# Exponential and inverse root of the attention stage on ScalarE, from one function table

## The reference, cut to what matters

```python
qk = x @ Wqk + bqk
v = x @ Wv + bv
scores = jnp.sum(qk[dst] * qk[src], axis=-1) / jnp.sqrt(jnp.float32(D))
scores = jnp.clip(scores, -5.0, 5.0)
m = jax.ops.segment_max(scores, dst, num_segments=N)
e = jnp.exp(scores - m[dst])
s = jax.ops.segment_sum(e, dst, num_segments=N)
attn = e / s[dst]
out = jax.ops.segment_sum(attn[:, None] * v[src], dst, num_segments=N)
out = out @ Wo + bo
h = out + x
mu = jnp.mean(h, axis=-1, keepdims=True)
var = jnp.mean(jnp.square(h - mu), axis=-1, keepdims=True)
return gamma * (h - mu) / jnp.sqrt(var + 1e-05) + beta
```

## Time and profile before

| | us |
|---|---|
| median of 3 runs | 3318.11 |
| lowest, highest | 3316.03, 3324.59 |
| the profiled execution | 3321.51 |
| its span, first to last instruction | 3319.7 |

### The profile page before, as it was taken

The page is one execution under the profiler, slowest core; times in us unless marked ns, Lnnn a source line. Parts: engine busy times, 40 slices in busy tenths (PEclk is TensorE's granted clock), DMA queues, the critical chain, the costliest instruction groups (busy, mean ns, idle before and its releaser), DMA issues. The chain is left out here.

```text
span 3319.7 us, 49065 instructions
## 1 busy us (share of the span) xinstructions
PE 2144.1 (65%) x10561; PEld 1502.5 (45%) x10561; DVE 2130.9 (64%) x8721; ACT 1682.1 (51%) x4589; POOL 1599.9 (48%) x1491
## 2 busy tenths in 40 slices
PE   0267353563775878777772777777885777773665
PEld 0123242252553656666650333333444666662555
DVE  1268842332886889898875777776754444441999
ACT  0149310122886556565654988988974444440222
POOL 0130046643001788888845655655515777775000
PEclk9779677777998677676775999999997888785999
DMA  7930142244999778787855999988985555541998
GB/s 312 346 103 6 48 86 37 69 115 90 325 325 315 250 240 245 239 251 237 247 131 159 284 270 278 295 266 262 301 197 188 186 186 184 181 158 71 312 317 283
DMA packets 494699, 696.78 MB, mean 210 GB/s; under 512 B 66363, under 2 KB 357398, under 8 KB 485932
## 3 DMA queue, kind: packets, MB, share of 16 engines
q1 hardware_dynamic: 414254, 485.35, 47.1%
q0 software_dynamic: 63360, 130.75, 14.8%
q10 hardware_dynamic: 16896, 78.91, 6.3%
HBM read 394.91 MB, written 327.18 MB: 218 GB/s over the span
## 5 line engine op out<-in xcount | busy, mean ns | idle before, releaser
L262 POOL DMA_INDIRECT xs<-x_d,table_src x400 | 385.2, 963 | 379.4 <-DVE x L1485 148.2
L262 POOL DMA_INDIRECT xs<-n_d,srcI x200 | 234.6, 1173 | 326.3 <-DVEq L1134 270.8
L262 POOL DMA_INDIRECT xd<-n_d,dstI x200 | 239.6, 1198 | 61.0 <-issue 54.9
L262 POOL DMA_INDIRECT xd<-x_d,table_dst x200 | 211.0, 1055 | 65.1 <-issue 65.1
L1699 POOL DMA_INDIRECT r_d<-rd,out_row x200 | 196.8, 984 | 61.3 <-issue 59.1
L1640 PE MATMUL bank<-nmsg,same 128*128 128x128 f32 x400 | 100.6, 335 | 149.7 <-ACT sums L1572 92.5
L1640 PEld LDWEIGHTS bank<-nmsg,same 128*128 128x128 f32 x400 | 61.8, 195 | 286.2 <-ACT sums L1572 223.1
L1822 PE MATMUL bank<-xs,same 128*128 128x129 f32 x400 | 106.4, 355 | 129.1 <-DVE same L1764 68.3
L518 PE MATMUL bank<-mask,h 128*128 128x512 f32 x160 | 104.1, 810 | 131.8 <-DVE mask L856 79.5
L452 POOL DMA_INDIRECT sum_d<-add,to x40 | 63.7, 1593 | 240.5 <-ACT add L647 226.9
L238 DVE RECIPROCAL rs<-root 128x4 f32<-128x4 f32 (+3 forms) x253 | 51.8, 205 | 193.0 <-ACT root L257 178.6
(11 more groups left out here) (382 smaller groups left out, 7173.8 us busy)
## 6 DMA issues: line engine op xcount, KB each, us to landing
n_d<-T SPq DMA_DIRECT2D x98, 528.0 KB, 3.8
nt<-n_d SPq DMA_DIRECT2D x49, 1056.0 KB, 7.0
r<-r_d SPq DMA_DIRECT2D x98, 520.0 KB, 5.5
bc<-dst_d SPq DMA_DIRECT2D x170, 256.0 KB, 4.8
r_d<-nv SPq DMA_DIRECT2D x49, 528.0 KB, 8.1
v_d<-nv SPq DMA_DIRECT2D x49, 528.0 KB, 7.8
nv<-v_d SPq DMA_DIRECT2D x49, 528.0 KB, 4.1
x_d<-x SPq DMA_DIRECT2D x100, 256.0 KB, 4.0
```

What stands on the lines that cost most here:

```text
L262: pool.indirect_dma_start(out=out, out_offset=None, in_=table, in_offset=bass.IndirectOffsetOnAxis(ap=index, axis=0)).then_inc(s, 16)
```

## The change

GpSimd's power, its constant `base` and its wait for the scores go. ScalarE takes the exponential of the score (`exps`) from its tables. The root and VectorE's reciprocal are replaced by two activations on ScalarE: `logs`, Ln of D-th of the sum plus eps, and `inverses`, Exp of minus half of that. One table set that holds Exp and Ln is loaded at the stage's start in the place of that of the root. On ScalarE, `exps` and `logs` stand ahead of `weigh` and `inverses` behind it.

```diff
-        base = sb("base", [P, G])
...
-                    nc.gpsimd.memset(base[:, :], math.e)
...
-                    def exps(g, s):
-                        hold("pool", pool, score_ready, g + 2)
-                        nc.gpsimd.tensor_tensor(e[:, s, :], base[:, :], score[:, s, :], ALU.pow).then_inc(e_ready, 1)
-                    unrolled(NGE, [(exps, 3), (src_used, S8), (dst_used, S8), (rows, 0)], S8)
+                    unrolled(NGE, [(src_used, S8), (dst_used, S8), (rows, 0)], S8)
...
-                    pipeline(dve, NGE, [(nodes_biased, 1, -1), (denominator, 6), (inverse, 2, late), (attended, 6), (offset, 2, late),
+                    pipeline(dve, NGE, [(nodes_biased, 1, -1), (denominator, 6), (attended, 6), (offset, 2, late),
                                         (nodes_stats, 1, -1), (sames, 3), (biased, 6), (scores, 2), (stats2, 6), (indices, 1),
                                         (nodes_summed, 1, -1), (attended_summed, 6), (differences, 1, late), (times_gamma, 7),
                                         (squares, 1, late), (nodes_gamma, 2, -1), (total, 1, late), (added, 7),
...
-                    act.preload_act_table(ACT.Sqrt)
+                    act.preload_act_table_set("natural_log_exp_and_others")
...
+                    def exps(g, s):
+                        act.wait_ge(score_ready, g + 2)
+                        nc.scalar.activation(e[:, s, :], score[:, s, :], ACT.Exp).then_inc(e_ready, 1)
...
-                    roots = rooting(act, tmp, root, mixed, rooted)
+
+                    def logs(k, s):
+                        act.wait_ge(mixed, k + 1)
+                        nc.scalar.activation(root[:, s, :], tmp[:, s % 2, 2, :], ACT.Ln, bias=eps[:, :], scale=1.0 / D).then_inc(rooted, 1)
+
+                    def inverses(k, s):
+                        act.wait_ge(rooted, k + 1)
+                        nc.scalar.activation(rs[:, s, :], root[:, s, :], ACT.Exp, scale=-0.5).then_inc(inverted, 1)
...
                     pipeline(act, NGE, [(hdT_copy, 2), (total(0), 4), (normed, 7), (total(1), 4), (nodes_normed(0), 2, -1),
-                                        (total(2), 4), (nodes_normed(1), 2, -1), (attT_copy, 5), (total(3), 4), (weigh, 3),
-                                        (roots, 1, late)], S8)
+                                        (total(2), 4), (nodes_normed(1), 2, -1), (attT_copy, 5), (total(3), 4), (exps, 3), (logs, 1, late),
+                                        (weigh, 3), (inverses, 1, late)], S8)
```

## The result

The changed kernel takes 3336.95 us (median of 4 runs, 3334.32 to 3339.46) against 3317.07 for the kernel before: the ratio is 1.0051, with a 95% interval of 1.0027 to 1.0076. It is slower, by half a per cent. The forecast was 3297 us. In some sets of measurements every kernel, the kernel before included, took 8 to 10% longer, so a time of the experiments means something only beside the kernel before of its own set (3319 or 3320 us in the one kind, 3587 to 3654 in the other).

A forecast was written before the change was run, and what follows sets the result against it. GpSimd was taken as the bound at 13.16 us a group; 12.6 after the change saves 21 us in 38 steady groups and 3 in the others, less 3 of drain: 3297 us, forecast span 3283 to 3308, eight in ten 3268 to 3335.

The forecast's parts named there:

- GpSimd loses the power, floor 12.3 us a group: GpSimd in attention: 13.16 us a group, less 1.09 for the power, plus 0.2 for gathers meeting VectorE operations more often.
- Product at m+2.5, at half clock m+2.8: TensorE's product start, counted from m, the end of L233 (mixed): 1.5 us later than the m+0.97 before.
- Length of the path: From one mixed to the next through product, total(1) and node rows: 11.4 us at full clock, 14.6 at half.
- The share of half clock: Part of TensorE's product at half clock: 16%, round 11.9 us, taken as 12.0 to 12.2; with 54% it is 13.1.
- Rival 3: Slower: the later product falls mainly into half clock, deciding from 57%; at 75% +33 us, 3351 us; chance 0.13.
- Two loops coupled: GpSimd's 12.3 us and the product path's 12.1, coupled by eight buffers, give 12.6 us a group.
- Drain: Behind the last gather some five rounds wait for product and weigh, 0.5 us longer each: +3 us.
- Table loads, exps, logs and inverses: ScalarE: one table set and load serves both functions; the two added activations cost 0.4 us a group, at most 0.6.
- The total: Whole kernel: 21 us less, all from the attention stage, giving 3297 us on the median of 3318.1.

The follow-up runs named there:

- e1d: The changed kernel with weigh put back ahead of logs on ScalarE, fourth run: 3268.7 us beside 3320.0 for the kernel before, ratio 0.9838.
- e8: The changed kernel with TensorE's four bias pieces of the product moved ahead of the first total: 3259.3 us beside 3319.4, ratio 0.9823.
- b0: The kernel before, unchanged, run again for its trace: 3320.6 us beside 3319.4 (one run).
- e7: The kernel before without the bias product of the scores (half of the product): 3326.2 us beside 3319.4, ratio 1.0015.
- a0: The changed kernel itself, run again: 3731.6 us beside 3654.3 for the kernel before, ratio 1.0250.
- e1b: The changed kernel with weigh put back ahead of logs on ScalarE, a repeat: 3700.2 us beside 3654.3 for the kernel before, ratio 1.0132.
- e2: The changed kernel with the power (exps) put back on GpSimd: 3642.4 us beside 3587.0 for the kernel before, ratio 1.0230.
- e5: The kernel before with roots ahead of weigh on ScalarE and nothing else changed: 3648.1 us beside 3587.0, ratio 1.0245.

## Why the prediction was wrong

The mechanism was in it, with the right lengths at either clock; the size of one term was wrong, the share of half clock in the product, and with it which of two loops is the longer.

- **GpSimd loses the power, floor 12.3 us a group.** Right as far as it can be seen: in e1d and e8, where little holds GpSimd up, 37 groups pass in the 450 us from 1200 to 1650, 12.2 us each (34 in the kernel before, 13.2). The gathers last 1.16 and 1.21 us there against 1.23 before. In the changed kernel they last 1.04 us, with GpSimd waiting for x2 between them.
- **Product at m+2.5, at half clock m+2.8.** Right within 0.2 us: between 1200 and 1650 us it is m+2.3 in 17 rounds and m+2.7 to m+2.8 in the 16 at half clock. But the place before the change was read from one quick round (m+0.97); the median there is m+1.3, so some 1.2 us were added, not 1.5.
- **Length of the path.** Right: 11.4 us at the full clock and 14.6 at half were predicted. The round with 4.17 us of product took 12.6 (11.4 with the 0.86 us that its product is longer gives 12.3; total(1), too, is at half clock there), and the one at half clock, 1315.93 to about 1330.4, took 14.4.
- **The share of half clock: wrong, and this is the failed step.** I took 16%, from the busy time of L1292 in the kernel before, as "of this very operation", "with a little for the product's later place". By the same working the changed kernel has (2.68 - 1.93)/(3.04 - 1.93) = 68%. With it the forecast's own formula gives 11.4 + 0.68 x 3.2 = 13.6 us, and measured are 13.5. Rival 3 (chance 0.13) had the point (57%) and the mechanism. The 54% of the stretch's mean clock was nearer than the row that I preferred. The rounds say the same: the product takes 5.65 us in 16 of 33 rounds between 1200 and 1650 us, and in 2 of 35 in the kernel before. The 16% came from one execution (b0 gives 25% and 7 of 35) with the product at its old place, and I carried it over to another place.
- **Two loops coupled.** I took 12.6 us, half a step above the longer of 12.3 and 12.1. With 13.6 the coupling no longer matters: GpSimd waits for x2 in 34 groups of the 500 us and follows.
- **Drain: +3 us forecast, +9 measured.** From the end of the last gather to that of the last x2 it was 46.2 us and is 55.5 (1723.9 to 1779.4). At the end of the last gather eight groups lack their x2 in the changed kernel, and seven in the kernel before.
- **Table loads, exps, logs and inverses.** Right: one load, and 0.20, 0.30 and 0.20 us. The Trainium skill, "ScalarE: Activation LUTs", section "What ACT_TABLE_LOAD costs", gives an estimate of 0.19 and 0.20 us for exps and inverses by its formula; the trace agrees, with 0.198 and 0.196.
- **The MLP stage: -12.6 us, not forecast.** Both traces of the kernel before, and e7, have it at 741 to 743 us, and the four of kernels without the power under the same conditions at 724 to 730. Its code is the same, and so are the busy times of VectorE (511 and 512 us) and ScalarE (590 and 591) in it, so it lies in waits. What does it is open.
- **The total: near the working by luck.** With 68% in the place of 16% the prediction's own working gives (13.6 - 13.16) x 50 = 22 us more than before, 3340 us, and 3337 were measured. But attention grew by 29.8 us, 20.5 up to the end of the last gather and 9.3 in the drain, and the MLP stage took 12.6 of it back. For the attention stage the forecast of -21 us was off by 51.

That the late product bounds the changed kernel (theory A) is shown by e1d (the order back: -68 us) and e8 (half of the product off the path, order unchanged: -78 us), with e7 as the control. Why the product falls into half clock is not shown. In the two rounds above TensorE stood idle 1.4 us for weigh, began the first product at the full clock and lost it in the middle of it; in the second it had stood idle as long and was at half clock. e1d, whose product starts some 0.7 us earlier, has 32% by the same working. That an earlier start goes with a lower share of half clock is what these numbers say, with 16 and 25% in the two traces of the kernel before, where it starts another 0.5 us earlier; they do not say why.

## What to carry to other kernels

In a hand-ordered queue, putting a waiting instruction one place earlier moves everything behind it, so follow the engine's queue into the next step and see what the latest of those feeds. Here a product of another engine that starts some 1.2 us later, and is at half clock more often, cost more than the power that left GpSimd was worth. A duration of TensorE that was read at one place of the cycle, in one execution, need not hold at another: this product took 3.31 us at the full clock and 5.65 at half. Take the stage's mean clock as one end and work out at which share the sign turns. And what on the long path does not need the late operand can go ahead of it, into the idle time (e8).

## What the runs showed of the hardware

- Beside a kernel before of 3587 to 3654 us the mean granted clock of TensorE over the kernel before was 0.78 to 0.80, beside one of 3317 to 3320 us 0.81 to 0.83; one and the same chip gave 3587 and 3320. In the traces of both kinds the first two stages are equally long (798 to 807 and 259 to 263 us), while the last edge stage has 558 to 561 us in one kind and 710 to 730 in the other. The change cost 2.5% instead of 0.5% (a0), and weigh first gave back 1.2% (e1b against a0) instead of 2.1%. What causes it is open.
- GpSimd's gathers show no cost at a somewhat higher DMA rate: from 1200 to 1650 us e8 moved 260 GB/s against 244, with a busy share of the DMA engines of 0.84 against 0.79, and its gathers took 1.21 us on average against 1.23.
- The Ln and Exp pair in place of Sqrt and VectorE's reciprocal cost nothing that can be measured (e2 beside e5).
